# Strassen's products for the experts' gate and up projections, in one transformer-like chain on a single core

## The reference

```python
x = x + jnp.tanh(g_xattn[0]) * _L0_xattn_ref(_layernorm(x), ctx, Wq, Wg, bg, Wkv, Wo)      # linear attention
x = x + jnp.tanh(g_ffn[0])   * _L0_ffn_ref(_layernorm(x), proj1, b1, proj2, b2, gate_w)    # 512 -> 2048 -> 512, gelu
x = x + jnp.tanh(g_xattn[1]) * _L1_xattn_ref(_layernorm(x), ctx, mask)                     # softmax over 64 context rows
x = x + jnp.tanh(g_ffn[1])   * _L1_ffn_ref(_layernorm(x), gate_weight, gate_up_proj, down_proj, merge_groups, dominant)
...
# _L1_ffn_ref: 8 groups of 192 hidden columns, all groups for every token
probs = softmax(x @ gate_weight.T); top_val, top_idx = top_k(probs, 8); top_val /= sum(top_val)
w_tg = sum over k of top_val * onehot(merge_groups[top_idx])          # token x group
gate, up = split(einsum('th,goh->tgo', x, gate_up_proj[dominant]))    # 512 -> 8*192 each
y = einsum('tgi,ghi->tgh', silu(gate) * up, down_proj[dominant])
out = einsum('tg,tgh->th', w_tg, y)
```

## Time and profile before

| | us |
|---|---|
| median of 3 runs | 1870.97 (1870.21 to 1871.59) |
| the profiled execution, its own time | 1873.45 |
| its span in the trace | 1871.7, granted clock 0.996 |
| PE busy | 1831.1 (98%) |
| DVE busy | 995.4 (53%) |
| ACT busy | 499.8 (27%) |
| POOL busy | 318.6 (17%) |

### The profile page before, as it was taken

One profiled execution on the slowest core, in us unless ns is written; L12 is line 12 of the kernel. 1 busy time (PEld: TensorE's weight loads), 2 busy tenths in 40 slices (PEclk: granted clock), 3 DMA queues, 4 the chain that ended last, 5 costly groups with the idle time before them and its releaser, 6 DMA issues.

```text
span 1871.7 us, 24531 instructions
## 1 busy us (share of the span) xinstructions
PE 1831.1 (98%) x9496; PEld 897.6 (48%) x9496; DVE 995.4 (53%) x2036; ACT 499.8 (27%) x745; POOL 318.6 (17%) x299
## 2 busy tenths in 40 slices
PE   8699999999999999999999999999999999999999
PEld 3445555544444444444444454544444444545444
DVE  5667777754555455553526453636455454546322
ACT  2324534311221221222112232222222222223211
POOL 1122322312012020202200011111111111111111
PEclk9989999999999999999999999999999999999999
DMA  4123443243323333240310200202020202010010
GB/s 159 51 65 123 140 130 102 91 131 78 102 69 105 109 79 107 68 109 1 90 51 12 86 31 18 82 18 77 20 75 12 88 12 82 18 46 24 18 51 29
DMA packets 145174, 129.01 MB, mean 69 GB/s; under 512 B 76642, under 2 KB 93154, under 8 KB 145058
## 3 DMA queue, kind: packets, MB, share of 16 engines
q1 hardware_dynamic: 145058, 127.45, 22.7%
HBM read 94.78 MB, written 32.64 MB: 68 GB/s over the span
## 4 chain that ended last, share of the span: by engine, by line
PE 83%; issue 7%; DVE 4%; DMA 2%; POOL 2%; ACT 1%; POOLq 0%; SPq 0%; DVEq 0%; ACTq 0%
PE bank L962 43%; PE bank L1051 17%; PE bank L1131 11%; PE bank L1031 4%; PE bank L971 3%; PE bank L1016 1%; PE bank L997 1%; POOL arena L936 1%; DMA arena<-x_after_ffn 1%; DVE arena L1317 1%; DVE arena L1384 1%; PE bank L1066 1%; PE bank L1093 1%; POOL arena L910 0%; DMA arena<-in_L_xattn_Wkv 0%
## 5 line engine op out<-in xcount | busy, mean ns | idle before, releaser
L962 PE MATMUL bank<-arena 128*128 128x512 f16 x4608 | 1044.4, 379 | 6.0 <-DVE arena L1338 3.9
L962 PEld LDWEIGHTS bank<-arena 128*128 128x128 f16 x4608 | 449.4, 98 | 526.4 <-DVE arena L1338 4.3
L1051 PE MATMUL bank<-arena 128*128 128x512 f16 x1536 | 352.1, 379 | 1.6 <-DVE arena L1545 1.6
L1131 PE MATMUL bank<-arena 128*128 128x512 f16 x1152 | 264.3, 379 | 0.9 <-POOL arena L936 0.9
L1051 PEld LDWEIGHTS bank<-arena 128*128 128x128 f16 x1536 | 150.0, 98 | 181.5 <-DVE arena L1545 2.1
L1230 ACT ACTIVATE arena<-bank,arena 128x512 f32<-128x512 f32 x128 | 99.5, 777 | 486.1 <-PE bank L962 482.6
L936 POOL TENSOR_TENSOR arena<-arena 128x512 f16<-128x512 f32 x96 | 111.0, 1156 | 671.7 <-ACT arena L1267 650.2
L1687 DVE SCALAR_TENSOR_TENSOR arena<-bank,arena 128x512 f32<-128x512 f32 x96 | 71.9, 749 | 273.9 <-PE bank L962 273.9
L1543 DVE TENSOR_SCALAR arena<-arena 128x512 f16<-128x512 f32 x128 | 73.5, 575 | 270.6 <-ACT arena L1230 270.6
L1131 PEld LDWEIGHTS bank<-arena 128*128 128x128 f16 x1152 | 112.6, 98 | 133.9 <-POOL arena L936 1.4
L1267 ACT ACTIVATE arena<-arena 128x512 f16<-128x512 f32 x96 | 60.4, 629 | 371.7 <-DVE arena L1699 371.7
(11 more groups left out here) (159 smaller groups left out, 1148.1 us busy)
## 6 DMA issues: line engine op xcount, KB each, us to landing
arena<-in_L_ffn_proj SPq DMA_DIRECT2D x64, 256.0 KB, 2.9
arena<-group_weights SPq DMA_DIRECT2D x64, 256.0 KB, 3.1
arena<-in_L_ffn_gate_up_proj SPq DMA_DIRECT2D x96, 96.0 KB, 2.0
x_after_attention<-arena SPq DMA_DIRECT2D x8, 1024.0 KB, 5.2
arena<-x_after_attention SPq DMA_DIRECT2D x8, 1024.0 KB, 5.5
x_after_ffn<-arena SPq DMA_DIRECT2D x8, 1024.0 KB, 4.3
arena<-x_after_ffn SPq DMA_DIRECT2D x8, 1024.0 KB, 7.5
arena<-in_x SPq DMA_DIRECT2D x7, 1024.0 KB, 5.5
```

What stands on the lines that cost most here:

```text
L962: m = e.matmul(bank[b][:, :], wT[l][:, c, tile * P:(tile + 1) * P], y[h][:, c, :], start=n == 0, stop=n == NPASS - 1)
L1051: m = e.matmul(bank[t][:, :], hv[h][:, 0, t * P:(t + 1) * P], w2T[l][:, j, :], start=j == 0 and i == 0, stop=j == NH - 1 and i == 2)
L1131: m = e.matmul(bank[t][:, :], hv[h][:, 0, t * P:(t + 1) * P], dnT[l][:, j, :], start=j == 0 and i == 0, stop=j == NR - 1 and i == 2)
```

## The change

Gate and up projections of a tile become one product with a 2 by 2 structure. The contraction (512 features) is cut in halves, the tokens in halves (HT = 256), and the outputs in gate and up. Strassen's form (Winograd's variant) makes the four quarters out of 7 products instead of 8; each product is 6 matmuls (3 passes by 2 contraction tiles) of 256 columns.

- Weights: for each quarter of the hidden rows (two tiles) seven forms (F_A11 to F_S1) are made, in high and low parts: scaled copies and high parts on ACT (fsplit, fhi), sums and low parts on POOL (flo, flo2). wsplit and wlo of gate and up fall away. Five of six quarters are made in stage F, the sixth in block 0 of stage E, as are the down weights' splits (wsplit on ACT, wlo on DVE; in the list `finer`, beside the list of attention tasks).
- Tokens: four sums of quarters of the normalised tokens (T_1 to T_4) are made for each block, in two halves: tsum and tlo on POOL, thi on ACT. The turns of layer norm M are now `mturn`: two copies on ACT and the subtraction on POOL.
- A step of stage E is now, in order: `mix` of the step before; p16 (2 products, bank 4); quarter 0 of dn two steps back; a task; p45 (2 products, bank 5); quarter 1 of dn; a task; mhi of the step before; p23 (2 products, bank 6); a task; p7 (1 product, bank 4); quarters 2 and 3 of dn; a task. All attention tasks share bank 7.
- The sums of the products are made by DVE: p16 (a copy of one half by ACT, then an addition of 256 columns), p45 (256), p23 (512, then silu on ACT), p7 (256, then 512), and mix (the product with silu, 512). POOL multiplies with the groups' weights, ACT makes the high part and POOL the low part.
- The tasks are spread: `slow` puts an empty place between some, the four reads are four tasks, and a block has 48 places (4 by 12). Beside the last block of stage F there are three places a step instead of two.

```diff
+    def second_tasks(i):
+        ph, b = i
+        slow = [None] if b > 0 else []
...
+        if ph == "L":
+            return [stats, *slow, norm(0), norm(1), turn(0, 2), *slow, turn(1, 3), *slow, turn(2), *slow, turn(3)]
+        def sums(p):
+            return [lambda: add("tsum", b, p), lambda: add("thi", b, p), lambda: add("tlo", b, p)]
+        return [stats, *slow, norm(0), norm(2), turn(0, 1), *slow, turn(2, 3), *slow, *sums(0), *slow,
+                turn(1), *slow, turn(3), *slow, sums(1)[0], lambda: add("router", b, banks=1), *sums(1)[1:]]
...
+        return [L[0], both(split, L[1] or (lambda: None)), *L[2:], lambda: add("scores", b, banks=1), *pause,
+                lambda: add("pturn", b, banks=1), *pause[1:], *[read(t) for t in range(NT)], *M,
+                *pause, lambda: add("rturn", b, banks=1), *pause,
+                lambda: add("gsum", b, banks=1), groups]
...
+            if side and J >= total - NH:
+                beside()
...
+    P_.ring, P_.turn = [7], 0
...
+    for s in range(total + 2):
+        b, j = divmod(s, NR)
+        if s < total:
+            if j == 0 and b == 0:
+                finer = finish_weights()
+            if j == 0 and b + 1 < NB:
+                side = attention_tasks(b + 1)
+        if 1 <= s <= total:
+            add("mix", s - 1)
...
+        if s < total:
+            add("p16", s, at=4)
+        down(s - 2, (0,))
+        apart()
+        if s < total:
+            add("p45", s, at=5)
+        down(s - 2, (1,))
+        apart()
+        if 1 <= s <= total:
+            add("mhi", s - 1)
+        if s < total:
+            add("p23", s, at=6)
...
+        apart()
+        if s < total:
+            add("p7", s, at=4)
+        down(s - 2, (2,))
+        down(s - 2, (3,))
         apart()
...
+        def product(out, j, f, y, c0, col):
+            n = 0
+            for h, l in PASSES:
+                for c in range(2):
+                    m = e.matmul(out, forms_of[j // 2][l][:, c, f, (j % 2) * P:(j % 2 + 1) * P],
+                                 y[h][:, c0 + c, col:col + HT], start=n == 0, stop=n == 2 * len(PASSES) - 1)
+                    n += 1
+            return m
...
+                product(bank[k][:, 0:HT], j, F_A11, yT[b % 2], 0, 0)
+                product(bank[k][:, HT:TOK], j, F_S2, tT[b % 2], 2 * T_2, 0).then_inc(p16_mm)
...
+            elif kind == "p16":
+                w.wait_ge(p1_ok, s + 1)
+                e.tensor_tensor(u_s[s % 2], bank[bank_of[step, 0]][:, HT:TOK], gate_s[s % 2][:, 0:HT], ALU.add).then_inc(c_ok)
+            elif kind == "p45":
+                w.wait_ge(p45_mm, s + 1)
+                e.tensor_tensor(gate_s[s % 2][:, HT:TOK], bank[bank_of[step, 0]][:, HT:TOK], u_s[s % 2],
+                                ALU.add).then_inc(c_ok)
+            elif kind == "p7":
+                w.wait_ge(p7_mm, s + 1)
+                e.tensor_tensor(u_s[s % 2], bank[bank_of[step, 0]][:, 0:HT], u_s[s % 2], ALU.add).then_inc(c_ok)
...
+                e.tensor_tensor(prod_s[s % 2].rearrange("p (h n) -> p h n", h=2),
+                                bank[bank_of[("p45", s), 0]][:, :].rearrange("p (h n) -> p h n", h=2),
+                                u_s[s % 2].unsqueeze(1).to_broadcast([P, 2, HT]), ALU.add).then_inc(c_ok)
+            elif kind == "p23":
+                w.wait_ge(p23_mm, s + 1)
+                e.tensor_tensor(gate_s[s % 2], bank[bank_of[step, 0]][:, :], gate_s[s % 2], ALU.add).then_inc(c_ok)
+            elif kind == "mix":
+                w.wait_ge(silu, s + 1)
+                e.scalar_tensor_tensor(out=prod_s[s % 2], in0=prod_s[s % 2], scalar=inv["up"], in1=gate_s[s % 2],
+                                       op0=ALU.mult, op1=ALU.mult).then_inc(prod)
...
+                if pairs > 0:
+                    w.wait_ge(t_lo, pairs)
...
+                e.activation(y_slot(t), block4(bank_of[step, 0]), ACT.Copy).then_inc(mt_copy)
+                w.wait_ge(mt_copy, n)
+                e.activation(y_of(i)[0][:, :, cols], y_slot(t), ACT.Copy).then_inc(mt_hi)
...
+            elif kind == "p23":
+                w.wait_ge(c_ok, c_nth(s, "p23"))
+                e.activation(gate_s[s % 2], gate_s[s % 2], ACT.Silu, scale=inv["gate"]).then_inc(silu)
```

585 lines of the change are left out of this document (404 added, 181 removed).

## The result

| | before | after |
|---|---|---|
| median, us | 1871.28 (1870.21 to 1873.31, 4 runs) | 1946.32 (1944.90 to 1947.83, 4 runs) |
| ratio, 95% interval | | 1.040 [1.0382, 1.0418] |
| span of the profiled execution | 1871.7 | 1946.0 |
| PE busy | 1831.1 (98%) | 1809.7 (93%) |
| DVE busy | 995.4 (53%) | 1144.9 (59%) |

The direction was forecast, the size not: 1906 us was forecast, with 1926 as the upper end.

What follows compares the result with a forecast made beforehand. PE was taken as the bound, with DVE's queue order making it wait. Terms of -57 (PE), +67 (waits), +5 (POOL), +6 (clock), +11.5 (block 0), +4 (stage F), +1 (end) gave +37; forecast 1906 us, range 1868 to 1926.

Steps and rivals of the forecast that it cites:

- PE's saving: Stage E: 42 matmuls of 256 columns at 109 ns, a step 7.17 instead of 7.77 us, 57 us less.
- Rival 3: Weight loads set the pace of 256-column matmuls, 134 ns each: 1950 to 2005 us, chance 0.05.
- The list of waits in blocks 1 to 6: PE waits for DVE sums behind tasks, step by step: 9.6 us a block against 7.1 gained, +15 for six blocks.
- The clock: Clock falls behind the router's wait at 2.4 us each, up to 17 us; a third taken, +6.
- the router's wait: Step 9: DVE's router chain holds p23's and p7's sums, so PE waits 3.9 us a block, 3.9 to 5 with POOL's surcharge.
- rival 4: Clock falls behind every router and POOL's collisions are full: 1920 to 1930 us, chance 0.2.
- Stage F: Beside its last block, tasks without empty places make PE wait 0 to 8 us, 4 taken.
- Block 0: Start of stage E: block 1's tasks, late x, wlo splits, a clock fall and late weight forms, +14 us in sum.
- The late forms' term: Block 0, steps 4 to 7: 14 us of POOL work delays mhi and so dn, 2 to 10 us, 5 taken.
- rival 1: PE stays fed because chains run between DVE's additions without holding them: 1815 to 1850 us, chance 0.13.

Runs made afterwards that it cites:

- Run 2: Changed kernel with all tasks of blocks 1 to 7 spread, each in its own place, router's chain in three pieces: 1913.19 us, ratio 1.0215.
- run 8: Run 2's order with the router's product three places earlier and POOL's second half of sums behind its vector pieces: 1887.41 us, ratio 1.0089.
- run 11: Changed kernel with edits of runs 5, 7, 8, 9, some block 0 tasks moved, places ahead of p7's sum kept freer: 1851.87 us, ratio 0.9894.
- Experiment 1: Changed kernel with the router's DVE chain cut into three plan steps, products' sums between them, in blocks 1 to 7: 1916.11 us, ratio 1.023.
- Run 7: Changed kernel with seven empty places among the tasks beside the last block of stage F: 1944.17 us, ratio 1.0387.
- Run 5: Changed kernel with block 1's x and block 7's store issued ahead of the down-weight loads, splits four places later: 1950.94 us, ratio 1.0424.
- run 6: Changed kernel with two empty places between the last forms' POOL sums (flo) and ScalarE high parts (fhi), twice: 1948.27 us, ratio 1.0407.
- run 9: Changed kernel with the late weight tiles' four sums made by VectorE in their own place instead of POOL: 1942.14 us, ratio 1.0369.

## Why the prediction was right in direction and half the size

**PE's saving: right.** 109 ns a matmul and 7.17 us a step were measured as forecast. Rival 3 is out. The estimate made there from the Trainium skill (TensorE: Matmul & The Clock Gate, Back-to-back issue gap) would have given 134 ns; the trace disagrees at 256 columns too.

**The list of waits in blocks 1 to 6: right.** They waited 1.49 us in step 0 (forecast 1.8; 2.49 in one block of six), 1.49 in step 1 (1.5), 0.36 at the scores (0.6, and 0.4 behind them, which did not come), 1.30 in step 5 (1.2), 0.50 on POOL in steps 7 and 8 (0.2), and 3.71 at the router (3.9): 8.8 us of 9.6, and 9.8 with the ends of rows at the six waits. (The rows cited for the 0.25 us after which a result reaches DVE give 0.20; it moves no wait by more than 0.05 us.) Run 2 shows that these waits came from the order of the same work, and runs 8 and 11 that what is left of them follows what stands ahead of p7's sum.

**The clock: the term that failed most.** "The router's wait, 3.9 to 5, lies at that edge. A fall costs 2.4 us ... I take a third of that, +6." In all seven blocks the clock fell behind the router's wait, and cost 1.4 to 2.9 us, 13.6 instead of 6. In block 0 it fell behind the waits of 13.63, 3.65 and 4.05 us as well, and behind the one of 3.05 it fell 0.67 us later (six matmuls of 512 columns took 2.25 us from start to start instead of 1.30): another 8.8 us instead of 2.4. With the 5.4 in stage F, for which nothing was set, the clock took 27.7 us against 8.4: 19 of the 37 that were missing. The one row at 3.29 us without a fall was a poor guide. The first half of rival 4 (chance 0.2) was true, at 13.6 us and not its 17; the other half was not, in this order: the chain's two-input operations took 0.29 us, with one of 0.39. Experiment 1 points the same way: 11 of its 27 us in six blocks were no waits.

**Stage F: +17 instead of +4.** "The tasks are now without empty places: ... 0 to 8, I take 4." PE's waits there were 3.57, 0.52, 1.46, 0.80, 2.07 and 2.96 us, 11.4 in sum. Behind the first and the last the clock fell, 5.4 us in the stage by the same reckoning (behind the last, twelve matmuls of 512 columns took 5.01 us instead of 2.75). I had priced two places, with no clock, and four other places waited as well. Run 7 shows that empty places take 4.8 us of the 11.4 away.

**Block 0: 31 us of waits instead of some 22.** "Its statistics wait for x of block 1 ...; here it goes first, and 1 MB alone takes about 6." It did not go first. The eight down-weight tiles stood ahead of it on SP's queue with 11 issues of 0.96 us each; I had counted the bytes and not the issues. Run 5 shows that some 4 us of the first wait were this. The late forms' term, "2 to 10, I take 5", was about 7 (4.05 and 3.05), and by POOL's queue as forecast (runs 6 and 9), the second of them by way of ScalarE's fhi.

**What rival 1 says now.** PE stays fed if the chains run between the sums without holding them: this was given 0.13, with 1815 to 1850 us. The changed kernel's order does not allow it; run 11's, with the same arithmetic, does in the steady blocks and comes to 1851.9, just above that range, since block 0 and stage F still wait.

Three things stay open. How much of block 0's remaining loss is DVE's load there and how much is its order was not taken apart further. The 4.27 us POOL wait of run 11 in block 0 was not mended. And no run shows what decides whether the clock falls behind a given wait.

## What to carry to other kernels

When one engine is the bound and another one makes its sums in one ordered queue, read the slack of each sum (here 0.5 us at p7), and what may stand ahead of it; load shares say nothing (with DVE at 63% of stage E PE was idle for 90.7 us, with DVE at 72% of the steady blocks for 0.8). A wait of some 2 to 4 us on TensorE can have two prices, the wait and the clock behind it, so cutting a chain in pieces can pay back more than its wait (27 us for 16 in run 1). A wait that is removed in a crowded stretch moves to the next queue, as runs 2, 5, 7, 8 and 9 show: mend one and read again, and only the sum of mends tells what the order was worth.

## What the hardware showed that I had not expected

- The clock fell behind waits shorter than I had taken for safe: 2.25 us (twelve matmuls in 2.59 us, run 8). Nor does the length of a wait alone decide it: in run 8 the same wait of 2.25 us was followed by a fall in three blocks and by none in four, and behind 2.49 us, at the same place of the same block, the twelve matmuls took 1.48 us in the changed kernel and 2.74 in run 1, while before no fall came behind 3.29 us.
- The 11 issues of down-weight loads, whose addresses come from registers, shut SP's queue for 0.96 us each (10.60 us), a plain store of 1 MB for 0.39 us: the smaller transfer can shut it longer. It need not: over the kernel the 32 issues of this kind took 0.33 to 1.88 us, with a median of 0.46. What made these long no run shows.
- A two-input DVE operation beside POOL: 0.29 to 2.05 us for 128 columns, 0.43 to 1.36 us for 256. Both ended 0.15 and 0.28 us behind POOL's instruction, so the price is what is left of that instruction, and POOL's longest one (128x1024, 2.13 us) is the one to keep away from a chain.
